# A selected-attention kernel: index scores and top-8 rounds moved one tile ahead, index lists spread by DMA instead of TensorE, one-hots of 1024 columns in a ring of four

## What is computed

```python
q_i = (x @ idx_wq).reshape(B, L, 4, 64); k_i = x @ idx_wk
s_i = relu(einsum('bthd,bsd->bths', q_i, k_i))
I = einsum('bths,h->bts', s_i, idx_w)
I = where(local, inf, I); I = where(causal, -inf, I)     # local: the last 64 keys
_, idx = top_k(I, 96)
key_c, value = (c_kv @ W_uk)[idx], (c_kv @ W_uv)[idx]
kr_sel = (x @ W_kr)[idx]; key_r = pope(kr_sel, angles of the rank 0..95)
scores = (q_c . key_c + q_r . key_r) * scale
out = softmax(scores) @ value @ W_out
```

## Time and profile before

| | |
|---|---|
| runs | 1688.45, 1693.25, 1685.04 us; median 1688.45 |
| profiled execution | 1687.32 us, span 1685.5 us |
| granted TensorE clock, mean | 0.75 |
| busy, share of the span | PE 59%, PEld 36%, DVE 64%, ACT 37%, POOL 3% |
| chain that ended last | DVE 34%, PE 23%, issue 14%, ACT 8% |
| DMA | 56.06 MB in 48782 packets, 33 GB/s |
| instructions | 40231, of them PE 16160 matmuls and as many weight loads |

### The profile page before, as it was taken

The page is one execution under the profiler, slowest core; times in us unless marked ns, Lnnn a source line. Parts: engine busy times, 40 slices in busy tenths (PEclk is TensorE's granted clock), DMA queues, the critical chain, the costliest instruction groups (busy, mean ns, idle before and its releaser), DMA issues.

```text
span 1685.5 us, 40231 instructions
## 1 busy us (share of the span) xinstructions
PE 996.5 (59%) x16160; PEld 612.2 (36%) x16160; DVE 1075.6 (64%) x2522; ACT 625.7 (37%) x1370; POOL 43.3 (3%) x40
## 2 busy tenths in 40 slices
PE   4665674577546665476637667466737657363564
PEld 2443453344324253243424335244414335131112
DVE  4355452556589975455679985456769885434995
ACT  2443331365433331364634331254725331143220
POOL 0000000010000000011000000001000000020000
PEclk8666767598768797687857879678857888675676
DMA  3000000200112200110013200020012300201320
GB/s 120 2 8 8 10 2 9 57 5 5 40 45 80 55 3 9 30 37 8 6 55 76 83 1 3 14 52 9 2 59 74 84 2 4 54 10 52 79 71 7
DMA packets 48782, 56.06 MB, mean 33 GB/s; under 512 B 21200, under 2 KB 27344, under 8 KB 48400
## 3 DMA queue, kind: packets, MB, share of 16 engines
q1 hardware_dynamic: 48592, 53.42, 12.5%
HBM read 49.73 MB, written 3.67 MB: 32 GB/s over the span
## 4 chain that ended last, share of the span: by engine, by line
DVE 34%; PE 23%; issue 14%; ACT 8%; DMA 1%; DVEq 1%; SPq 1%; POOL 0%; ACTq 0%; POOLq 0%
DVE SG L1647 5%; PE bank L697 3%; PE bank L727 3%; DVE CV L1657 2%; PE bank L514 2%; DVE XP L1657 2%; DVE onehot L1430 2%; PE bank L808 2%; PE bank L853 2%; DVE Y L1734 2%; DVE big L1638 1%; PE bank L811 1%; DVE ml L1386 1%; PE bank L678 1%; ACT QBD L1019 1%
## 5 line engine op out<-in xcount | busy, mean ns | idle before, releaser
L697 PE MATMUL bank<-onehot,tparts 128*32 128x128 bf16 x7680 | 154.6, 240 | 72.0 <-DVE onehot L1430 43.0
L697 PEld LDWEIGHTS bank<-onehot,tparts 128*32 128x32 bf16 x7680 | 128.7, 107 | 107.3 <-issue 73.0
L1647 DVE TENSOR_TENSOR_SCAN SG<-big 128x512 f32<-128x512 f32 x128 | 149.0, 1206 | 4.5 <-ACT big L1156 0.8
L1430 DVE TENSOR_SCALAR onehot<-ib,CO 128x512 bf16<-128x512 f16 x320 | 99.0, 369 | 82.3 <-ACT ib L1026 75.2
L1026 ACT ACTIVATE ib<-bank 128x512 f16<-128x512 f32 x128 | 75.8, 596 | 147.1 <-PE bank L678 145.6
L853 PE MATMUL bank<-XP,CO 128*128 128x512 f32 x128 | 83.8, 790 | 58.3 <-DVE XP L1657 58.2
L853 PE MATMUL bank<-CV,CO 128*128 128x512 f32 x128 | 88.8, 831 | 45.9 <-DVE CV L1657 45.8
L983 ACT ACTIVATE relu_s<-bank,nml 128x192 f32<-128x192 f32 (+1 forms) x128 | 52.9, 425 | 162.8 <-DVE nml L1391 162.8
L1156 ACT ACTIVATE big<-DEL,Aneg 128x512 f32<-128x512 f32 x128 | 84.5, 716 | 55.1 <-DVE SG L1647 44.0
L727 PE MATMUL bank<-GT,QBD 128*32 128x32 f32 x3072 | 61.4, 214 | 48.6 <-DVE G L1440 32.6
L514 PE MATMUL bank<-CO,relu_s 128*128 128x128 f32 (+2 forms) x256 | 49.1, 356 | 69.3 <-ACT relu_s L983 69.3
(11 more groups left out here) (307 smaller groups left out, 2012.0 us busy)
## 6 DMA issues: line engine op xcount, KB each, us to landing
BC<-bc_rows SPq DMA_DIRECT2D x128, 256.0 KB, 4.4
big<-comb_rows SPq DMA_DIRECT2D x8, 1024.0 KB, 9.9
rows_bounce<-RO SPq DMA_DIRECT2D x256, 8.5 KB
W<-w SPq DMA_DIRECT2D x1, 2818.0 KB, 14.2
RB<-rows_bounce SPq DMA_DIRECT2D x16, 136.0 KB, 2.1
X<-x SPq DMA_DIRECT2D x4, 256.0 KB, 2.9
out<-CV SPq DMA_DIRECT2D x4, 256.0 KB, 2.3
big<-w SPq DMA_DIRECT2D x1, 576.0 KB, 7.8
```

The costliest lines, as they stand in the source:

```text
L697: m = mm(bank[2 + c % 2][32 * bb:32 * bb + 32, at:at + P], tparts[:, kt, part, 32 * kind:32 * kind + 32], chosen[:, kt, bb, :, :], start=( ...
L1430: m = TS(onehot[:, r % 2, kt, :], ib[:, r % 2, :], co("pos")[:, kt:kt + 1], None, ALU.is_equal)
L1647: m = dve.tensor_tensor_scan(hs[:, j, :], dA[:, n % 2, j, :], dBu[:, n % 2, j, :], 0.0, ALU.mult, ALU.add)
```

## The change

What it does:

- The index scores of tile i+1 are computed in tile i: TensorE puts heads 0 and 1 ahead of the first pick and heads 2 and 3 behind the first chunk, in banks 0 and 1, which the list products no longer use. The last two wait for the relu of the first two. Only tile 0 of a row has its own at its start. ScalarE's relus stand behind the query spread and ahead of the second chunk's copy.
- VectorE sums the heads of tile i+1 after the last `turned` of tile i, and has its rounds 0 and 1 of top eight behind the differences and the sums of the picked scores; round 2 stands ahead of the rotation and round 3 behind `merge_a`. In tile 0 of a row the sum and rounds 0 to 2 all stand ahead of the rotation.
- The list is no longer turned. SyncE stores `idxh` to DRAM (`idx_rows`), waits, and loads it back repeated to all partitions in four pieces, one for each chunk, in phase 3 of the tile.
- A one-hot covers a whole chunk, 1024 columns, for one key tile; four of them form a ring, each with its own signals to and from TensorE. A pick matmul has 256 columns instead of 128.
- For the room: `PT`, `QS`, `QBT`, `CT` and `idxT` are gone and use `PR`, `q_e`, `XT` and `XD`; VectorE's rotation waits for TensorE's last reading of `PR`.

The diff, cut to its core:

```diff
+def round_of(i, c, kt):
+    return 2 * i * (i + 1) + c * (i + 1) + kt
...
-        ib = sb("ib", [P, 2, 4 * P], F16)
-        onehot = sb("onehot", [P, 2, NT, 4 * P], BF16)
+        ib = sb("ib", [P, 4, 8 * P], F16)
+        onehot = sb("onehot", [P, 4, 8 * P], BF16)
...
@@ sync: tiles
-                    for _ in range(TILE_PHASES - 1):
+                    for _ in range(3):
+                        yield
+                    sp.wait_ge(idx_ok.sem, idx_ok.at(b, i + 1))
+                    sp.dma_start(idx_rows[i % 2].rearrange("(q j) -> q j", j=NREM), idxh[:, :]).then_inc(idx_st.sem, idx_st.up())
+                    sp.wait_ge(idx_st.sem, idx_st.at(b, i + 1))
+                    of_chunk = idx_rows[i % 2].rearrange("(b c x) -> c b x", b=4, c=4)
+                    for c in range(4):
+                        sp.dma_start(ib[:, c, :].rearrange("p (b x) -> p b x", b=4),
+                                     of_chunk[c].unsqueeze(0).to_broadcast([P, 4, 2 * P])).then_inc(ib_in[c].sem, ib_in[c].up())
+                    for _ in range(TILE_PHASES - 4):
                         yield
@@ tensor: tiles
-                    for h in range(NIH):
-                        o = 64 * (h % 2)
-                        mm(bank[h][:, 0:Wi], QI[o:o + 64, h // 2, i * P:(i + 1) * P], KI[o:o + 64, 0:Wi],
-                                      start=True, stop=True).then_inc(ix_ps.sem, ix_ps.up())
-                    pe.wait_ge(ix_relu.sem, ix_relu.at(b, 4 * i + 1))
...
+                    def pick(c):
+                        if c >= 2:
+                            pe.wait_ge(g_sb.sem, g_sb.at(b, 4 * i + c - 1))
+                            pe.wait_ge(gt_ok.sem, gt_ok.at(b, 4 * i + c - 1))
+                        else:
+                            pe.wait_ge(pl_ok.sem, pl_ok.at(b, 2 * i + 2))
+                        for kt in range(i + 1):
+                            n = round_of(i, c, kt)
+                            pe.wait_ge(oh_ok.sem, oh_ok.at(b, n + 1))
+                            for kind in range(2):
                                 for part in range(3):
                                     for bb in range(4):
+                                        m = mm(bank[2 + c % 2][32 * bb:32 * bb + 32, 256 * kind:256 * kind + 256],
+                                               tparts[:, kt, part, 32 * kind:32 * kind + 32],
+                                               onehot[:, n % 4, 256 * bb:256 * bb + 256],
...
+                            m.then_inc(oh_used.sem, oh_used.up())
-                    spread(0)
                     local_out(1)
-                    spread(1)
+                    if i < NT - 1:
+                        for h in range(2):
+                            index_scores(i + 1, h, h)
                     local_rows(1)
...
                     for c in range(4):
-                        pick(2 * c)
-                        if c < 3:
-                            spread(2 * c + 2)
-                        pick(2 * c + 1)
-                        if c < 3:
-                            spread(2 * c + 3)
+                        pick(c)
+                        if c == 0 and i < NT - 1:
+                            for h in range(2, 4):
+                                pe.wait_ge(ix_relu.sem, ix_relu.at(b, 4 * i + 3 + h))
+                                index_scores(i + 1, h, h - 2)
                         yield
@@ scalar: tiles
-                    spread(0)
-                    spread(1)
                     local_out_t(1)
                     spread_query()
+                    if i < NT - 1:
+                        for h in range(2):
+                            index_relu(i + 1, h, h)
@@ vector: tiles
+                    if i == 0:
+                        index_sum(0)
+                        top8(0, 0)
+                        top8(0, 1)
+                    top8(i, 2)
                     yield
...
-                    top8(0)
+                    top8(i, 3)
+                    CP(idxh[:, :], idx[:, :]).then_inc(idx_ok.sem, idx_ok.up())
...
+                    def onehots(c):
+                        dve.wait_ge(ib_in[c].sem, ib_in[c].at(b, i + 1))
                         for kt in range(i + 1):
+                            n = round_of(i, c, kt)
+                            if n >= 4:
+                                dve.wait_ge(oh_used.sem, oh_used.at(b, n - 3))
+                            TS(onehot[:, n % 4, :], ib[:, c, :], co("pos")[:, kt:kt + 1], None, ALU.is_equal).then_inc(oh_ok.sem, oh_ok.up())
...
                     turned(3)
+                    if i < NT - 1:
+                        index_sum(i + 1)
```

More of the change, by code:

```diff
@@ L216, in build @@
         XD = sb("XD", [DTR + 2 * DS, L])
+        CT = XD[0:NE, :]
         DEL = sb("DEL", [P, 2, L])
@@ L282, in build @@
         idx_ok = signal("idx_columns_ready", NT)
-        ib_ps = signal("idx_spread_in_psum", 8 * NT)
-        ib_sb = signal("idx_spread_in_sbuf", 8 * NT)
-        oh_ok = signal("onehot_round_ready", 8 * NT)
-        g_round = signal("rows_round_in_psum", 8 * NT)
+        idx_st = signal("idx_rows_stored", NT, 16)
+        ib_in = [signal(f"idx_spread_ready_chunk_{c}", NT, 16) for c in range(4)]
+        oh_ok = signal("onehot_round_ready", round_of(NT, 0, 0))
+        oh_used = signal("onehot_round_picked", round_of(NT, 0, 0))
         g_sb = signal("picked_latents_ready", 4 * NT)
@@ L569, in tiles, with index_scores @@
                     c0 = 96 - W0
+                    def index_scores(t, h, k):
+                        o, Wt = 64 * (h % 2), index_width(t)
+                        mm(bank[k][:, 0:Wt], QI[o:o + 64, h // 2, t * P:(t + 1) * P], KI[o:o + 64, 0:Wt],
+                           start=True, stop=True).then_inc(ix_ps.sem, ix_ps.up())
                     if i == 0:
                         pe.wait_ge(kt_sb.sem, kt_sb.at(b, 1))
+                        for h in range(NIH):
+                            index_scores(0, h, h)
+                        pe.wait_ge(ix_relu.sem, ix_relu.at(b, 1))
                     else:
@@ L666, in tiles @@
                     yield
-                    def spread(r):
-                        if r < 2:
-                            pe.wait_ge(pt_sb.sem, pt_sb.at(b, 2 * i + 2))
-                            pe.wait_ge(idx_ok.sem, idx_ok.at(b, i + 1))
-                        else:
-                            pe.wait_ge(ib_sb.sem, ib_sb.at(b, 8 * i + r - 1))
-                        for q in range(4):
-                            t = 4 * r + q
-                            m = mm(bank[r % 2][:, q * P:(q + 1) * P], idxh[:, t:t + 1].to_broadcast([P, P]),
-                                   ident_h[:, :], start=True, stop=True)
-                        m.then_inc(ib_ps.sem, ib_ps.up())
@@ L1340, in rotate, with index_sum @@
                     dve.wait_ge(done.sem, done.now(b))
[L1342 to L1347 removed]
+                def index_sum(t):
+                    Wt = index_width(t)
+                    dve.wait_ge(ix_relu.sem, ix_relu.at(b, 4 * t + 1))
+                    TS(score[:, 0, 0:Wt], relu_s[:, 0, 0:Wt], w("idxw")[:, 0:1], None, ALU.mult).then_inc(ix_used.sem, ix_used.up())
@@ L1357, in tiles, with top8 @@
                     dve.wait_ge(vec.sem, vec.now(b))
+                def top8(t, r):
+                    Wt = index_width(t)
+                    cur, nxt = score[:, r % 2, 0:Wt], score[:, (r + 1) % 2, 0:Wt]
+                    dve.sem_inc(hold_dve, 1)
+                    dve.max(top[:, 8 * r:8 * r + 8], cur).then_inc(vec.sem, vec.up())
+                    dve.wait_ge(vec.sem, vec.now(b))
+                    dve.sem_inc(hold_dve, 1)
+                    m = dve.max_index(idx[:, 8 * r:8 * r + 8], top[:, 8 * r:8 * r + 8], cur)
+                    if r < 3:
+                        m = dve.match_replace(nxt, top[:, 8 * r:8 * r + 8], cur, NEG_TOP)
+                    m.then_inc(vec.sem, vec.up())
+                    dve.wait_ge(vec.sem, vec.now(b))
@@ L1358, in tiles @@
+                for i in range(NT):
+                    W0 = first_width(i)
+                    c0 = 96 - W0
+                    if i == 0:
+                        index_sum(0)
+                        top8(0, 0)
+                        top8(0, 1)
+                    top8(i, 2)
                     yield
                     dve.wait_ge(q_sp.sem, q_sp.at(b, i + 1))
+                    if i >= 1:
+                        dve.wait_ge(pbd_ps.sem, pbd_ps.at(b, i))
                     STT(out=muq[:, :, :].rearrange("p h c -> p (h c)"), in0=bank[0][:, 0:256], scalar=0.0,
```

116 lines of the change are left out of this document (35 added, 81 removed).

## The result

The changed kernel took **1589.54 us** in the median of 4 runs (1588.12 to 1590.30), the kernel before 1690.85 in its 4 runs beside it; the ratio is 0.9403, with a 95% interval of [0.9381, 0.9426]. Against the first median of before, 1688.45, that is 99 us less. The profiled execution has a span of 1588.5 us and lay 97.0 us under before's span. 1604 was forecast, range 1568 to 1650.

What follows compares the result with a forecast made beforehand. Woven tiles 0 and 1 were taken as handover chains, tile 2 and the first third of tile 3 as VectorE's queue. Row 0's 23 us plus woven rows' 59, rounded to 83 with a set-up copy, gave 1687.3 - 83 = 1604 us, range 1568 to 1650.

Steps and rivals of the forecast that it cites:

- Start of a tile: Row 0, tiles 1 to 3: query matmul goes first; of a 6.9 us lead 2.6 is left, as returning rows are late.
- The picks, row 0: Row 0's picks without list matmuls and copies: tiles 0 to 3 win 3.0, 2.7, 6.9 and 9.5 us.
- I take the same clock: Picks of tiles 1, 2, 3 in row 0 keep TensorE's old granted clock of 0.81, 0.88 and 0.80.
- The issue stalls: TensorE's 26.9 us of stops inside picks, seemingly every 256 instructions or so, should nearly vanish with 256-column matmuls.
- rival 3: The issue stalls in the picks stay, giving 18 us back: 1622 us, chance 0.06.
- Woven rows: Rows 1 to 3: tiles 0 to 3 win 4, 4.5, 5.2 and 6 us, 19.7 a row, 59 us in all.
- the three moved rounds at nothing: Top-eight rounds moved into the tile before, at most 2 us each at 448 columns, cost nothing outside the scan.
- New transfers: SyncE's list store and four 256 KB loads per tile land by about 10 us, inside 12.4 us of cover: cost nothing.
- the fourth rival: Lists land 20 us late, each of 16 tiles waits some 7.5 us: slower, 1724 us, chance 0.04.
- Rival 1: The rest of the row before paces the woven tiles; only 41 us won: 1646 us, chance 0.20.
- Rival 5: TensorE's new wait behind the query spread gives back some 3 us in each of eight tiles: 1628 us, chance 0.08.
- Rival 2: All named list waits, relu waits and issue stalls go, nothing replaces them; 152 us won: 1535 us, chance 0.10.

Runs made afterwards that it cites:

- e1: Changed kernel with each 256-column matmul of the picks split into two of 128 columns again; 1632.66 us, ratio 0.9689.
- e13: The changed kernel, unedited, run again beside later runs on the same chip; 1589.31 us, ratio 0.9410.
- e12: Changed kernel with three more waited-for loads of the list's first piece ahead of its four loads, so lists land late; 1593.60 us, ratio 0.9441.
- e3: Changed kernel with ScalarE's relus of the next tile's heads 0 and 1 moved ahead of the query spread; 1586.34 us, ratio 0.9413.

## Why the prediction was right

The direction, the places and most signs held; the time was 14.5 us under the forecast, inside the range. That it came so near is in part luck, since errors cancel, most of all in the woven rows. (The range's lower edge, 119 us, is 1.43 times the sum and not "a third more".) By its steps:

- **Start of a tile.** Right: the returning rows were late next. The forecast had VectorE's merge wait 1 to 2 us in tiles 1 to 3 of row 0, and it waited 1.7, 1.7 and 2.5:

```profile
91.92 0.17 DVE L1299 TENSOR_TENSOR mj<-ml,RB 128x8 f32<-128x8 f32 x1 [1.71 <-DMA RB<-rows_bounce]
...
140.18 0.17 DVE L1299 TENSOR_TENSOR mj<-ml,RB 128x8 f32<-128x8 f32 x1 [1.67 <-DMA RB<-rows_bounce]
...
191.50 0.17 DVE L1299 TENSOR_TENSOR mj<-ml,RB 128x8 f32<-128x8 f32 x1 [2.48 <-DMA RB<-rows_bounce]
```

  The starts (to the first local maximum) gave 1.5 us for the 2.6 forecast. The rows landed 9.0, 8.9 and 9.7 us after the tile's start, where 8.8 was worked out; that takes up 1.2 us of the forecast's gain.
- **The picks, row 0.** Mis-sized, in tiles 2 and 3. From the last local exponential to the picked scores the four tiles won 2.9, 3.1, 10.1 and 13.7 us; forecast 3.0, 2.7, 6.9 and 9.5. The step that failed is "I take the same clock", with the busy time got by subtracting the lists alone. The picks of tiles 2 and 3 ran at a granted clock of 1.00 and 0.86 for 0.88 and 0.80. Scaled by that, the forecast's 10.9 and 15.2 us become 9.6 and 14.1; measured 9.8 and 12.3. What is left in tile 3, 1.8 us, is about what e1 shows for width (12.1 against 10.6). That the picks' higher clock comes from their being without gaps is not shown: e1, with gaps, had 1.00 and 0.91, and e13, the changed kernel again, 0.92 and 0.85 in its windows; there tiles 2 and 3 won 9.2 and 12.2 us. So the clock of such a stretch is partly chance, while busy time times clock in tile 3 is 10.6 in both.
- **The issue stalls.** Right that they go (none is left, under 8 us was forecast) and that they come at 256 instructions. Undersized: rival 3 priced them at 18 us, e1 at 43. In the tiles that it counted (tiles 2 and 3 of row 0, the woven tiles 3) the stops are 18.6 us in 16 places in the old trace and 28.0 in 18 in e1: about as many, but longer. That waits for lists had given the supply time before would fit, but is not shown. And the forecast took columns to cost the same in either width. VectorE has its like: one-hots of 1024 columns were to cost "the same per column", and took 0.49 us in the mean where two of 512 took 0.74, so its busy time with them fell from 99.0 to 72.6 us.
- **Woven rows.** The sum was near (forecast 19.7 a row; measured 24.3, 24.7 and 14.3), its parts were not. Tile 0 was to win 4 and won 1.8, -0.8 and -4.2: the step costed "the three moved rounds at nothing", by the waits of VectorE after the picked scores as row 0 has them. In the woven rows the experts' steps are queued behind them. Tile 1 was to win 4.5 and won 10.5, 7.4 and 4.0, since it gets that work done for it. Tile 2: 5.2 forecast, 0.5, 3.3 and 6.1 measured. Tile 3: 6 forecast, 11.5, 14.8 and 8.4 measured, the largest error; the picks' of row 0 would fit, which is not shown. So 59 forecast and 63 measured agree by luck: tiles 0 together gave 15 us less than forecast and tiles 3 gave 17 more.
- **New transfers.** Right for the forecast: no one-hot waits for a DMA in the changed kernel. But in tile 0 of rows 1 to 3 the first piece landed 19 to 21 us behind the cast, as late as the fourth rival supposed, and cost nothing, because the first one-hot there came 24 to 25 us behind it. The rival's price was wrong. It has every tile pay from 12.4 us on, and its 17.6 us is where that reaches the 83 us of the sum; by it, first pieces at 16.5 us (e12, tile 2 of row 0) would cost some 66 us, and e12 lost 4. The leads differ by tile (12 us from cast to first one-hot in tiles 1 to 3 of row 0, 22 to 37 in the woven rows), and a one-hot that comes late does not hold up TensorE while that has other work.
- **The rivals.** Rival 1 (the rest paces the woven tiles) is false by 63 us won there. Rival 5 (the new wait behind the query spread) is false: the wait exists, 4.5 us in eight places, and without it e3 was no faster. Rival 2 lost to the new waits named above, VectorE's for the local scores first.

## What to carry to other kernels

Small matmuls are also bounded by how fast their instructions arrive: count instructions between two real waits, and if 256 of them run in less than some 4 us (the supply here), make each do more before looking at anything else. Stops counted in an old trace may not be all that such an edit is worth: here the wide form was also cheaper by the column. Work moved ahead into another tile's idle time is not free where engines run fixed programs: it is paid by what is queued behind it there, and an engine relieved of it may only wait longer for another.

## What the runs showed of the hardware that was not expected

- TensorE's instructions came at 256 per 3.6 to 4.0 us (e1), each block with a packet of 16384 bytes on q8, and the picks of the changed kernel, at 3.75 us for a block at a clock of 1.00, are no slower than that. Whether fewer instructions elsewhere would pay, such as the 3072 matmuls of 32 columns in L729 (10.1 us of issue before them), was not tried.
- A store of 8 KB issued on SyncE at 286.6 us, 1.4 us behind two loads of a megabyte each, let its loads start at 298.2, 11.6 us later; the same happened in tile 0 of rows 2 and 3 (11.5 and 11.7), and elsewhere the same store took 1.4 to 1.5. Here the list had 25 us, so it cost nothing:

```profile
285.14 1.32 SPq L481 DMA_DIRECT2D big<-comb_rows  x2
286.59 0.53 SPq L445 DMA_DIRECT2D idx_rows<-idxh  x1
298.18 2.02 SPq L449 DMA_DIRECT2D ib<-idx_rows  x4
```
